# Layer 1 of a two-layer attention kernel: coefficients and first combination behind the output's copy, scores copied in a pair, low halves later in GpSimd's order

## What is computed

```python
xn = layernorm(groupnorm(x)) * ln_w + ln_b           # per token, 192 channels
Q, K, V = xn @ Wq.T, xn @ Wk.T, xn @ Wv.T
S = Q @ K.T                                          # 4096 x 4096 for each image
attn = e1/(e1+e2) * softmax(S) + e2/(e1+e2) * relu(S)**2
x = x + attn @ V + x_in                              # with the layer's own residual
```

## Time and profile before

| | |
|---|---|
| median of 3 runs | 3560.64 us (3558.88 to 3561.38) |
| the profiled execution | 3561.09 us, its span 3559.3 us |
| busy over the span | PE 3188.6 us (90%), ACT 2096.1 (59%), DVE 1988.1 (56%), POOL 1019.1 (29%) |
| weigh groups, L1372 (high and low) | 546.8 and 504.6 us |
| scores, L1359 | 639.2 us |
| low halves, L1132 | 551.9 us, 256 of 2.17 us on average |
| combinations, L1642 | 209.3 and 206.8 us, 256 of 1.67 us on average |
| maxima, L1606 | 327.2 us |

### The profile page before, as it was taken

One profiled execution on the slowest core, in us unless ns is written; L12 is line 12 of the kernel. 1 busy time (PEld: TensorE's weight loads), 2 busy tenths in 40 slices (PEclk: granted clock), 3 DMA queues, 4 the chain that ended last, 5 costly groups with the idle time before them and its releaser, 6 DMA issues. The chain is left out here.

```text
span 3559.3 us, 48038 instructions
## 1 busy us (share of the span) xinstructions
PE 3188.6 (90%) x16424; PEld 1279.7 (36%) x16424; DVE 1988.1 (56%) x2522; ACT 2096.1 (59%) x2306; POOL 1019.1 (29%) x510
## 2 busy tenths in 40 slices
PE   1239999999999999999999966899999858999998
PEld 0012232222322323223222222455555424555555
DVE  4655243752257432563420145688888555888886
ACT  0015655556556565564666612688888415888886
POOL 1210202102021020020200003366566432666565
PEclk9669999999999999999999988999999979999999
DMA  6131212212103111131110033477777724877777
GB/s 179 45 77 28 60 42 45 57 45 55 50 24 77 44 37 50 35 78 32 25 44 7 10 90 92 102 139 146 145 143 139 159 75 99 145 138 144 145 144 132
DMA packets 691175, 295.71 MB, mean 83 GB/s; under 512 B 603314, under 2 KB 645042, under 8 KB 689266
## 3 DMA queue, kind: packets, MB, share of 16 engines
q1 hardware_dynamic: 690996, 293.45, 38.7%
HBM read 95.46 MB, written 34.28 MB: 36 GB/s over the span
## 5 line engine op out<-in xcount | busy, mean ns | idle before, releaser
L440 ACT ACTIVATE prob<-ps_s,cur 128x1024 f32<-128x1024 f32 x1024 | 1084.5, 1110 | 738.4 <-PE ps_s L514 736.8
L527 PE MATMUL ps_a<-prob,vt 128*64 128x512 f32 x4096 | 997.2, 608 | 0.0
L1132 POOL TENSOR_TENSOR p_lo<-gp,p_hi 128x1024 f16<-128x1024 f32 x256 | 551.9, 2166 | 402.9 <-ACT p_hi L1231 397.8
L1359 PE MATMUL ps_s<-kst,qs 128*128 128x512 f16 x2560 | 639.2, 383 | 20.3 <-DMA qs<-q_scratch 12.1
L1372 PE MATMUL ps_o<-v_hl,at_hi 128*128 128x384 f16 x2048 | 546.8, 328 | 28.4 <-DMA at_lo<-p_lo 26.9
L508 PE MATMUL ps_s<-q_a,k_a 128*128 128x512 f16 x2048 | 535.1, 383 | 7.6 <-issue 2.6
L1372 PE MATMUL ps_o<-v_hl,at_lo 128*128 128x192 f16 x2048 | 504.6, 247 | 0.0
L1606 DVE TENSOR_SCALAR_CACHE_REDUCE neg<-ps_s,mix 128x1024 f32<-128x1024 f32 x256 | 327.2, 1278 | 131.7 <-PE ps_s L1359 130.4
L527 PEld LDWEIGHTS ps_a<-prob,vt 128*64 128x64 f32 x4096 | 249.4, 136 | 412.4 <-issue 410.3
L1359 PEld LDWEIGHTS ps_s<-kst,qs 128*128 128x128 f16 x2560 | 244.8, 99 | 247.0 <-issue 23.3
L508 PEld LDWEIGHTS ps_s<-q_a,k_a 128*128 128x128 f16 x2048 | 138.0, 97 | 517.1 <-ACT prob L440 437.2
(11 more groups left out here) (176 smaller groups left out, 2763.2 us busy)
## 6 DMA issues: line engine op xcount, KB each, us to landing
z<-z_scratch SPq DMA_DIRECT2D x96, 384.0 KB, 3.9
sq<-rn_scratch SPq DMA_DIRECT2D x16, 768.0 KB, 10.6
qs<-q_scratch SPq DMA_DIRECT2D x64, 128.0 KB, 2.8
gn_x<-in_x SPq DMA_DIRECT2D x4, 1536.0 KB, 18.7
z_scratch<-gn_x SPq DMA_DIRECT2D x4, 1536.0 KB, 11.6
q_a<-hi SPq DMA_DIRECT2D x64, 96.0 KB, 2.4
rden<-den_scratch SPq DMA_DIRECT2D x64, 96.0 KB, 2.2
o_scratch<-o_s SPq DMA_DIRECT2D x64, 96.0 KB, 1.9
```

The lines of the kernel that those rows point to most:

```text
L440: act.activation(prob[:, a % PR, :], ps_s[:, a % 2, :], ACT.Exp, bias=cur[:, slot:slot + 1], scale=1.0 / SPLIT).then_inc(exped, 1)
L527: ins = pe.matmul(ps_a[h * HALF:(h + 1) * HALF, j % 2, :], vt[:, slot, m, :], prob[:, a % PR, h * CH:(h + 1) * CH], start=(m == 0), stop=( ...
L1132: pool.tensor_tensor(p_lo[:, cols], prob[s][:, cols], p_hi[:, cols], ALU.subtract).then_inc(lo_made[c], 1)
L1359: ins = pe.matmul(ps_s[:, c % 2, h * CH:(h + 1) * CH], qs[:, s, qt, :], kst[:, ktile, cols], start=(t == 0), stop=(t == len(terms) - 1))
```

## The change

Only the orders of three queues in the row loop change, and one wait is added. GpSimd: the cast of chunk 2 goes to ScalarE, that of chunk 0 comes from ScalarE, the lows are issued in the order of chunks with that of chunk 0 now written in the next slot, and low 1 also waits for combination 2. ScalarE: square 0 ahead of `factors`, squares 3, 1 and 2 in a block with the cast of chunk 3 of the row before among them, relus 0 and 1 and exps 0 and 1 in pairs. VectorE: `coefficients` and combination 0 directly behind `copy_output`, maxima 0 and 1 as a pair behind them, combination 3 at the slot's end.

```diff
@@ GpSimd, low(row, s, c) and slot(t, s) @@
                         pool.wait_ge(hi_made[c], RB * b + row + 1)
+                        if c == 1:
+                            pool.wait_ge(p_made[2], RB * b + row + 1)
                         pool.tensor_tensor(p_lo[:, cols], prob[s][:, cols], p_hi[:, cols], ALU.subtract).then_inc(lo_made[c], 1)
 
                     def slot(t, s):
+                        low(t - 1, 1 - s, 0)
                         high(t - 1, 1 - s, 1)
                         low(t - 1, 1 - s, 1)
-                        high(t - 1, 1 - s, 2)
+                        low(t - 1, 1 - s, 2)
                         low(t - 1, 1 - s, 3)
-                        low(t - 1, 1 - s, 2)
-                        low(t, s, 0)
+                        high(t, s, 0)
@@ ScalarE, slot(t, s) @@
                         exp_piece(t, s, 3)
+                        square(t, s, 0)
                         factors(t, s)
-                        square(t, s, 0)
+                        square(t, s, 3)
+                        high(t - 1, 1 - s, 3)
+                        square(t, s, 1)
+                        square(t, s, 2)
                         relu(t + 1, 1 - s, 0)
-                        square(t, s, 3)
-                        square(t, s, 1)
+                        relu(t + 1, 1 - s, 1)
                         exp_piece(t + 1, 1 - s, 0)
-                        high(t, s, 0)
-                        square(t, s, 2)
-                        relu(t + 1, 1 - s, 1)
-                        high(t, s, 3)
                         exp_piece(t + 1, 1 - s, 1)
                         relu(t + 1, 1 - s, 2)
                         exp_piece(t + 1, 1 - s, 2)
+                        high(t, s, 2)
                         relu(t + 1, 1 - s, 3)
@@ VectorE, slot(t, s, j) @@
                         copy_output(t - 2, s)
-                        maximum(t + 1, 1 - s, 0)
                         coefficients(t, s)
                         combine(t, s, 0)
-                        combine(t, s, 3)
+                        maximum(t + 1, 1 - s, 0)
+                        maximum(t + 1, 1 - s, 1)
                         combine(t, s, 1)
-                        maximum(t + 1, 1 - s, 1)
                         maximum(t + 1, 1 - s, 2)
                         combine(t, s, 2)
                         add_output(t - 2, s, j)
                         maximum(t + 1, 1 - s, 3)
+                        combine(t, s, 3)
```

## The result

The changed kernel takes 3592.5 us (median of 4 runs, 3589.5 to 3594.4) against 3559.8 for the kernel before beside it: ratio 1.0092, 95% interval 1.0075 to 1.011. It is 0.9% **slower**, where 11 us less had been forecast.

The account below looks back on a forecast made before the run. TensorE, busy 99.00 of 100 us in the row loop, was taken as the bound. A steady gain of 11.3 less 0 for head and drain, off the median 3560.64, gave 3549.4 us, range 3546 to 3568.

Parts of the forecast that it names:

- the stall of before: In every second slot TensorE waited for chunk 1's late low transpose: weigh group 2 began at 5.70 instead of 5.42.
- the lock: Between VectorE and GpSimd on SBUF: the first to issue holds it for its whole instruction, the other waits.
- rival 1: Chance 0.18, slower: past 5.86 low 3 locks before combination 0, and TensorE waits 1.9 us at the fifth score half.
- factors at nothing: On ScalarE: square 0 ahead of factors costs nothing, factors being ready at 3.78 and coefficients starting at 3.83.
- the loop's turn on VectorE: A gap of about 0.4 where VectorE's hardware loop turns, in slots that begin an iteration; taken as 0.
- the ring: VectorE and GpSimd handing the lock to and fro around a slot: 16.63 against TensorE's 16.78, shorter by 0.15.
- the margins: Slack of four things TensorE waits for, such as copy_output and the fifth score half: 1.0 or more, all positive.
- lost slot: A slot where low 3 takes the lock before combination 0 and TensorE stands for 1.9.
- the price of a loss: TensorE standing for 1.9 each time; at 56 / 6 losses 18 us, net +7, 3567.
- The ceiling: Most the steady slots could gain: 11.8 us, or 11.3 with a slot of 16.78.
- Head and drain: Filling the pipeline at an image's start and emptying it at the end: 0 together, from -1.5 (a gain) to +4.

Follow-up runs that it names:

- run 4: The kernel before with only low 1's wait for combination 2 added: 3544.7 us (median of 4), ratio 0.9955.
- run 7: The changed kernel with factors ahead of square 0 again: 3585.7 us (one run).
- run 3: The changed kernel with ScalarE's cast of chunk 3 placed one square later: 3562.8 us (one run).

## Why the prediction was wrong

*Right: the stall of before.* The contended combination 2, the late store and the transposes behind it were the cause; run 4 shows it. *Right: the lock*, both ways, and the place, the wait (1.95 against 1.9) and the deciding point of rival 1 (5.86 against 5.87). *Right: factors at nothing* (run 7), and the loop's turn on VectorE is hidden: no pair of slots shows it.

**The step that failed is the sum of the ring: 16.63 against a slot of 16.78.** From the slot beginning at 2421.51 in the changed kernel, VectorE and then GpSimd:

```profile
2426.85 1.28 DVE L1644 SCALAR_TENSOR_TENSOR gp<-gp,coef,rn 128x1024 f32<-128x1024 f32 x1
...
2431.11 1.28 DVE L1644 SCALAR_TENSOR_TENSOR gp<-gp,coef,rn 128x1024 f32<-128x1024 f32 x1 [0.15 <-DVE neg L1608]
```
```profile
2419.62 4.22 POOL L1134 TENSOR_TENSOR p_lo<-gp,p_hi 128x1024 f16<-128x1024 f32 x2 [1.23 <-DVE gp L1644]
...
2430.08 1.04 POOL L1125 CAST p_hi<-gp 128x1024 f16<-128x1024 f32 x1
...
2436.60 4.23 POOL L1134 TENSOR_TENSOR p_lo<-gp,p_hi 128x1024 f16<-128x1024 f32 x2 [1.23 <-DVE gp L1644]
```

Low 2 ends at 2423.84 and, one turn of the ring later, at 2440.83. Link by link:

| link | predicted | measured |
|---|---|---|
| end of low 2 to combination 0 (combination 3, copy_output, coefficients) | 2.88 | 3.01 |
| combination 0, low 3, cast 0 | 4.28 | 4.26 |
| combination 1 | 1.09 | 1.28 |
| low 0, cast 1, combination 2 | 4.09 | 4.07 |
| to low 1 | 0.07 | 0.14 |
| lows 1 and 2 | 4.22 | 4.23 |
| sum | 16.63 | 16.99 |

Two links carry 0.32 of the 0.36. Combination 1 was taken as waiting at the lock, where it ends 1.09 after its partner; in fact it is asked for just as the cast ends (2431.11 and 2431.12) and takes its whole 1.28. What holds it is VectorE's own queue, which the sum left out: combination 0 and the two maxima take 4.26 from 2426.85, as long as combination 0, low 3 and the cast. And copy_output with the step behind it takes 0.96, not 0.82: I had subtracted an overlap that no row showed, and reckoned the same link at 0.87 where the margins were worked out. The slot was off the other way. The gapless slot in the earlier trace rows still held 0.08, the weigh group behind the turn at 1.06 where the same group takes 0.98 without the stall, in slots of 16.69; the kernel before had single slots of 16.69, turn to turn, as well. A margin of +0.15 was in truth -0.30, and the forecast rested on its sign.

The prediction saw that a ring 0.2 too long would cost, and gave it one lost slot in six, net +7. With 0.3 it is 13 in 56, one in four. The second mis-sized term is the price of a loss: 2.12 only where the clock stays, 3.80 where it falls (below). 8 x 2.12 + 5 x 3.80 = 36.0 for the 13 long steady slots, and 970.7 - 56 x 16.69 = 36.1.

*The ceiling* was 16.3 (475.22 + 475.75 - 56 x 16.69), not 11.8, for the same 0.08. *Head and drain* were taken at 0, at most +4: they hold the other 12.2 of the 31.9. The end of image 1, from its last steady turn to its last, went from 41.4 to 46.5, with one more lost race in it. From there to image 2's first steady turn it went from 218.1 to 223.8, of which 3.7 lie ahead of the row loop, where no instruction changed. The whole stretch is 218.7 to 222.1 in the profiles of the eight runs, and longest in the changed kernel; what sets it stays open, and with it a few us of the result. The remaining 1.4 lie at the start of image 1 and the end of image 2.

## What to carry to other kernels

Two engines that hand one lock to and fro are one engine. Add up a whole turn of the ring, with what either does in between alone, and compare it with the slot of the engine that you mean to keep busy: if it is longer, by however little, the surplus either comes back in every slot (run 3) or piles up until an order tips, and then costs far more than it saved. For each link ask also when the engine's own queue lets it start. The sum here, of a dozen links, was off by 0.36, so a margin below that is no margin; take a link out (a copy, a wait) before you rely on it. And where one queued instruction meets one partner at the wrong time, try the one wait that parts them before you rewrite three queues.

## What the runs showed of the hardware

A wait of TensorE of 1.95 us lengthened the slot by 2.12 in some cases and by 3.80 in others. In both of the cases below TensorE waited, for 1.95 and 1.94 us, behind a steady stretch at full granted clock. The lines are the 5 us in which each wait ends, with the granted clock in the last column but two:

```profile
2325.00:2330.00 5.00, 4.16 (x15) 2.02 (x16) 3.54 (x5) 3.76 (x5) 3.77 (x3) 0.66 0.71 135
...
2396.00:2401.00 5.00, 4.59 (x29) 2.66 (x30) 4.25 (x7) 4.11 (x5) 3.36 (x3) 1.00 0.67 125
```
